# Four of sixteen window subtractions a step: from one GpSimd instruction to a negated copy and an accumulating DMA

## The reference

```python
disp = (x @ W_disp).reshape(B, T, nh, bd).transpose(0, 2, 1, 3)
disp_win = _windows(disp, delta)                        # delta = 64
strain = disp_win - disp[:, :, :, None, :]
bond_act = jax.nn.gelu(strain @ W_strain + rel_emb @ W_pos, approximate=False)
bond_logits = (bond_act @ W_bond)[..., 0]
damage_act = jax.nn.gelu(strain @ W_dmg + b_dmg, approximate=False)
damage = jax.nn.sigmoid((damage_act @ W_dmg_out)[..., 0] + b_dmg_out[0])
logits = bond_logits - 10.0 * damage
weights = jax.nn.softmax(logits, axis=-1)               # masked below the sequence's start
out = jnp.einsum('bntd,bntde->bnte', weights, val_win)
```

## Time and profile before

| | |
|---|---|
| median of three runs | 4021.71 us |
| the profiled execution | 4033.82 us, span 4032.3 us |
| VectorE busy | 3379.6 us, 84% of the span |
| ScalarE busy | 2576.9 us, 64% |
| TensorE busy | 2547.4 us, 63% |
| GpSimd busy | 2476.6 us, 61% |

### The profile page before, as it was taken

One profiled execution on the slowest core, in us unless ns is written; L12 is line 12 of the kernel. 1 busy time (PEld: TensorE's weight loads), 2 busy tenths in 40 slices (PEclk: granted clock), 3 DMA queues, 4 the chain that ended last, 5 costly groups with the idle time before them and its releaser, 6 DMA issues. The chain is left out here.

```text
span 4032.3 us, 64337 instructions
## 1 busy us (share of the span) xinstructions
PE 2547.4 (63%) x20970; PEld 1282.8 (32%) x20970; DVE 3379.6 (84%) x4350; ACT 2576.9 (64%) x1812; POOL 2476.6 (61%) x1748
## 2 busy tenths in 40 slices
PE   5661556766666666668888864565666656565556
PEld 3440112322222222246667631122222222222224
DVE  6886999999999999923433369999999999999993
ACT  1111878888788887833333356777777777777773
POOL 1222887668787787813333467677767767676762
PEclk9885878888888888879999987777878787878886
DMA  7883121322222222127887841222222222222222
GB/s 258 304 304 99 37 74 63 96 81 78 72 70 84 91 80 75 58 79 235 243 243 240 244 139 32 68 65 74 64 75 64 75 64 75 64 75 64 74 63 81
DMA packets 376227, 445.81 MB, mean 111 GB/s; under 512 B 49185, under 2 KB 291697, under 8 KB 376050
## 3 DMA queue, kind: packets, MB, share of 16 engines
q1 hardware_dynamic: 293106, 283.77, 22.4%
q0 software_dynamic: 58752, 148.46, 11.3%
q10 hardware_dynamic: 24192, 11.02, 1.0%
HBM read 239.08 MB, written 204.02 MB: 110 GB/s over the span
## 5 line engine op out<-in xcount | busy, mean ns | idle before, releaser
L1198 PE MATMUL ps_l<-u_dve,wsel 128*32 128x512 f32 x6144 | 1004.0, 780 | 1001.8 <-ACT u_dve L1003 640.7
L1102 DVE SCALAR_TENSOR_TENSOR u_dve<-s_win,rpos,ps_here 128x512 f32<-128x512 f32 x1792 | 1225.8, 737 | 74.3 <-PE ps_here L1181 51.4
L1003 ACT ACTIVATE u_dve<-u_dve 128x4096 f32<-128x4096 f32 x224 | 809.9, 3616 | 427.8 <-DVE u_dve L1102 427.0
L947 POOL TENSOR_TENSOR u_pool<-s_win 128x4096 f32<-128x4096 f32 x128 | 1021.9, 7983 | 9.7 <-PE ps_l L1198 6.9
L1097 DVE TENSOR_TENSOR u_dve<-s_win,ps_here 128x4096 f32<-128x4096 f32 x160 | 703.0, 4409 | 0.0
L1198 PEld LDWEIGHTS ps_l<-u_dve,wsel 128*32 128x32 f32 x6144 | 211.1, 128 | 1447.7 <-issue 647.1
L926 POOL DMA_INDIRECT xslot_dram<-xr,slot_now x512 | 520.0, 1016 | 154.1 <-issue 147.8
L935 POOL DMA_INDIRECT yg<-yslot_dram,slot_now x512 | 499.1, 975 | 164.6 <-issue 144.1
L1001 ACT ACTIVATE u_dve<-u_dve,bdmg_sb 128x4096 f32<-128x4096 f32 x128 | 474.6, 3708 | 91.5 <-DVE u_dve L1097 86.8
L1001 ACT ACTIVATE u_pool<-u_pool,bdmg_sb 128x4096 f32<-128x4096 f32 x128 | 473.7, 3701 | 27.7 <-POOL u_pool L947 27.5
L1391 DVE TENSOR_TENSOR hs<-sg,ps_e 128x512 f32<-128x512 f32 x168 | 115.4, 687 | 382.6 <-ACT sg L1376 382.6
(11 more groups left out here) (142 smaller groups left out, 3366.2 us busy)
## 6 DMA issues: line engine op xcount, KB each, us to landing
band<-band_dram SPq DMA_DIRECT2D x32, 2048.0 KB
xslot_dram<-zero SPq DMA_DIRECT2D x16, 2688.0 KB, 10.1
xs<-xslot_dram SPq DMA_DIRECT2D x168, 256.0 KB, 3.6
yslot_dram<-ys POOLq DMA_DIRECT2D x168, 256.0 KB, 3.2
band_dram<-ml SPq DMA_DIRECT2D x64, 512.0 KB
we<-in_w_expert SPq DMA_DIRECT2D x336, 64.0 KB, 2.8
s_win<-s_dram SPq DMA_DIRECT2D x64, 288.0 KB, 8.2
s_dram<-s_sb POOLq DMA_DIRECT2D x16, 1024.0 KB, 4.6
```

The source lines that it names most:

```text
L947: pool.tensor_tensor(item_buffer(n), windows(par, ty, d0, 8), s_win[:, par, ty, PAD:PAD + TC].unsqueeze(1).to_broadcast([P, 8, TC]), ALU.s ...
L1003: act.activation(u, u, ACT.Gelu).then_inc(gelu_done, 1)
L1102: last = dve.scalar_tensor_tensor(out=item_buffer(n)[:, d, :], in0=s_win[:, par, ty, d0 + d + 1:d0 + d + 1 + TC], scalar=rpos[:, d0 + d:d0 ...
L1198: last = pe.matmul(ps_l[32 * g:32 * g + 32, cgrp % 2, ty, :], wsel[:, ty, q, :], item_buffer(n)[:, d, :], start=(q == 0), stop=(q == 3))
```

## The change

GpSimd no longer subtracts. For items 3, 7, 11 and 15 it writes the negated own row 8 times into the item's buffer (a `tensor_scalar` with one SBUF input), waits for that write, and issues a DMA from SBUF to SBUF that adds the 8 shifted rows of `s_win` to what stands there. ScalarE waits for the DMA's semaphore instead of GpSimd's. The loads of the windows wait for `gelu_done` of the step before instead of the two subtraction counters. The rings keep their sizes (3 and 2).

```diff
-POOL_ITEMS = (3,)
+DMA_ITEMS = (3, 7, 11, 15)
+DVE_BUFS = 3
+DMA_BUFS = 2
...
-                            if some(ND * (2 * it + par - 1)):
-                                sp.wait_ge(sub_dve, ND * (2 * it + par - 1))
-                                sp.sem_inc(held, 1)
-                            if some(NPI * (2 * it + par - 1)):
-                                sp.wait_ge(sub_pool, NPI * (2 * it + par - 1))
+                            if some(NI * (2 * it + par - 1)):
+                                sp.wait_ge(gelu_done, NI * (2 * it + par - 1))
                                 sp.sem_inc(held, 1)
...
-                                pool.tensor_tensor(
-                                    item_buffer(n), windows(par, ty, d0, 8),
-                                    s_win[:, par, ty, PAD:PAD + TC].unsqueeze(1).to_broadcast([P, 8, TC]),
-                                    ALU.subtract).then_inc(sub_pool, 1)
+                                if some(NI * s + buffer_free(par, n)):
+                                    pool.wait_ge(item_done, NI * s + buffer_free(par, n))
+                                    pool.sem_inc(held, 1)
+                                u = item_buffer(par, n)
+                                pool.tensor_scalar(
+                                    u, s_win[:, par, ty, PAD:PAD + TC].unsqueeze(1).to_broadcast([P, 8, TC]),
+                                    -1.0, None, ALU.mult).then_inc(base_set, 1)
+                                pool.wait_ge(base_set, NM * s + k + 1)
+                                pool.sem_inc(held, 1)
+                                pool.dma_start(u, windows(par, ty, d0, 8), accum_op=ALU.add)\
+                                    .then_inc(sub_dma[landed(it, par, n)[0]], 16)
...
-                                if n % 4 in on_pool:
-                                    if some(NPI * s + pool_of[n]):
-                                        act.wait_ge(sub_pool, NPI * s + pool_of[n])
+                                if n in DMA_ITEMS:
+                                    i, count = landed(it, par, n)
+                                    act.wait_ge(sub_dma[i], count)
                                 else:
-                                    if some(ND * s + dve_of[n]):
-                                        act.wait_ge(sub_dve, ND * s + dve_of[n])
+                                    act.wait_ge(sub_dve, ND * s + dve_of[n])
```

More of the change, by code:

```diff
@@ L655, in moe_attention_layer @@
         win_loaded = [sem(f"win_loaded{g}") for g in range(HG)]
-        sub_dve, sub_pool, gelu_done, item_done = sem("sub_dve"), sem("sub_pool"), sem("gelu_done"), sem("item_done")
+        sub_dve, gelu_done, item_done = sem("sub_dve"), sem("gelu_done"), sem("item_done")
+        base_set, sub_dma = sem("base_set"), [sem(f"sub_dma{i}") for i in range(DMA_BUFS)]
         tanh_done, logits_in = sem("tanh_done"), sem("logits_in")
@@ L681, in attend @@
             chunk0 = (1 - half) * NCH // 2 - it0
-            u_dve = sb(f"u_dve_{half}", [P, 3, 8, TC], F32, c)
-            u_pool = sb(f"u_pool_{half}", [P, 2, 8, TC], F32, c)
+            u_dve = sb(f"u_dve_{half}", [P, DVE_BUFS, 8, TC], F32, c)
+            u_dma = sb(f"u_dma_{half}", [P, DMA_BUFS, 8, TC], F32, c)
             s_win = sb(f"s_win_{half}", [P, HG, 2, SW], F32, c)
@@ L709, in attend, with slot_of @@
             ps_u = c.enter_context(nc.psum_tensor(f"ps_u_{half}", [P, TC], F32))
[L710 to L714, removed]
+            on_dve = [n for n in range(NI) if n not in DMA_ITEMS]
+            dve_of = [sum(q in on_dve for q in range(n + 1)) for n in range(NI)]
+            ND, NM = len(on_dve), len(DMA_ITEMS)
+            def slot_of(m):
+                par, n = m // NI % 2, m % NI
+                if n in DMA_ITEMS:
+                    return "dma", (par * NM + DMA_ITEMS.index(n)) % DMA_BUFS
+                return "dve", (par * ND + on_dve.index(n)) % DVE_BUFS
             def steps(e, step):
@@ L738, in windows, with item_buffer, buffer_free, landed @@
                 return bass.AP(row.tensor, row.offset, [list(row.ap[0]), [1, nd], [1, TC]])
-            def item_buffer(n):
-                if n % 4 in on_pool:
[L743 to L750, removed]
+            def item_buffer(par, n):
+                which, i = slot_of(par * NI + n)
+                return (u_dma if which == "dma" else u_dve)[:, i]
+            def buffer_free(par, n):
+                m = par * NI + n
+                back = next(k for k in range(1, 2 * NI + 1) if slot_of(m - k) == slot_of(m))
+                return n - back + 1
+            def landed(it, par, n):
+                i = slot_of(par * NI + n)[1]
+                uses = [m for m in range(2 * NI) if slot_of(m) == ("dma", i)]
+                return i, 16 * (len(uses) * it + sum(m <= par * NI + n for m in uses))
             with nc.Block() as block:
@@ L1087, in step @@
                                     add_routed(s - first, 1 - par, 2 * n + d)
-                            if "i" in st and n % 4 not in on_pool:
+                            if "i" in st and n not in DMA_ITEMS:
                                 if dve_of[n] == 1:
@@ L1091, in step @@
                                     dve.wait_ge(here_done, s + 1)
-                                if some(NI * s + buffer_free(n)):
-                                    dve.wait_ge(item_done, NI * s + buffer_free(n))
+                                if some(NI * s + buffer_free(par, n)):
+                                    dve.wait_ge(item_done, NI * s + buffer_free(par, n))
                                 here = ps_here[:, ty, :]
                                 if ty or n in biased:
-                                    last = dve.tensor_tensor(item_buffer(n), windows(par, ty, d0, 8),
+                                    last = dve.tensor_tensor(item_buffer(par, n), windows(par, ty, d0, 8),
                                                              here.unsqueeze(1).to_broadcast([P, 8, TC]), ALU.subtract)
```

15 lines of the change are left out of this document (7 added, 8 removed).

## The result

The changed kernel takes 4600.19 us (median of 4 runs, 4591.94 to 4604.51), the kernel before takes 4021.43 us beside it: a ratio of 1.1442 [1.1426, 1.1458]. The forecast was 3883 us, its range 3777 to 4120; the kernel is slower by 14%, and slower than the range's end. Its profiled execution took 4604.27 us.

What follows compares the result with a forecast made beforehand. VectorE was taken to pace both halves. The profiled 4033.8 us - 245 (stalls) + 76 (half 1) + 29 (half 0) = 3894 us; the median runs 12 us lower, so 3883 was forecast, range 3777 to 4120.

Steps and rivals of the forecast that it cites:

- I take 3.6 us: the write has no second input to fetch, which puts it next to the memset: GpSimd's one-input write of 4096 elements, taken as 3.6 us, between a memset of 3.51 and the subtraction of 8.19.
- the 6 us that the prediction itself named as a sign of being wrong: A GpSimd write of over 6 us would show the forecast wrong.
- the write is no shorter: Rival, chance 0.06: GpSimd's write takes 7 to 8 us, stalls stay, landings come 4.4 us later; median 4197 us.
- The stalls: VectorE's two-input instructions wait 344 us for GpSimd's SBUF-reading instruction; the shorter write saves 71%, 245 us.
- The DMA: The accumulating DMA's time from issue to landing, L, taken as 16 us; upper bound near 23 us.
- lower bound: L if the second read is all that accumulation adds: 2.0 + 4 x 2.54 = 12.2 us.
- The estimate of 11.6 us: L from two skill pages, 2.0 + 9.6 us; with it the sum would be a gain of some 230 us.
- Right in mechanism in half 1: Late landing of item 3 delays VectorE's item 8 by 5.1 us in 15 steps of half 1: 76 us.
- the term "29 us": In even steps of half 0, item 7's late landing delays VectorE's item 12 by 4.1 us in 7 steps.
- GpSimd's DMA issues lie in the 4.6 us that its write gives back: Issuing the DMAs on GpSimd fits in the time its shorter write frees, so it costs nothing.
- VectorE's own stream was the same: VectorE's own instruction stream is unchanged by the edit, costed at nothing.
- late window: Window loads wait for Gelu, some 5 us later, costed at nothing; uncovered, VectorE's first item would start late by those 5 us.

Runs made afterwards that it cites:

- price list: Kernel before with single GpSimd operations on 128x4096 behind its end, each beside 8 VectorE additions: multiplication 11.0 us, copy 4.1, subtraction 7.5.
- no DMA: Changed kernel without the accumulating DMA, ScalarE waiting for GpSimd's write of the negated row: 4133.24 us, ratio 1.0279.
- late addition: Changed kernel with GpSimd's addition L978 at item 9 instead of item 5: 4518.68 us, ratio 1.1223.
- one item earlier: Each write and DMA issued one item earlier: changed kernel with its multiplication 4268.2 us; with the row negated once a step and copied 8 times 3736.85 us.
- the run in 4 pieces: Kernel before, no DMA, with GpSimd's subtraction cut into 4 instructions of 1024 elements: 4057.17 us, ratio 1.0116.
- the kernel with the copy: Changed kernel with a plain copy of the own row instead of the multiplication by -1: 3960.34 us, ratio 0.9849.

## Why the prediction was wrong

**The step that failed** is "I take 3.6 us: the write has no second input to fetch, which puts it next to the memset", with its bound above, "the two-input subtraction with 8.19 us". The write takes 10.6 us, outside both ends, and over the 6 us that the prediction itself named as a sign of being wrong. The bounds assumed that one input cannot cost more than two. The price list shows that it can: the kind of instruction decides (multiplication by a number 11.0 us, copy 4.1, two-input subtraction 7.5). The rival "the write is no shorter" had the direction, with a chance of 0.06 and a price of 4197; it priced later landings alone, with 8 us as the worst.

What the longer write does, as far as the runs show it, from the kernel before on:

- The write alone, 10.6 for 8.2 us: +114 us (no DMA), by way of stalls. The gates and the softmax line have 411.8 and 271.4 us there, 119 more than in the earlier trace rows; L1148 gives 42 back, and two lines that the prediction did not count, the mask's addition (L1131 before) and the copy of `slot_now`, add 45.
- The DMA behind it: 467 us more, by way of waits. In the changed kernel VectorE's idle time ahead of L1120 is 389.1 us, of which TensorE's late release is 288.7; the rest of its new idle time stands mostly ahead of the softmax (L1153 and L1160, 64 us each).
- Of this, the place of L978 is 82 us (late addition), and all that an earlier issue removes 332 us (4600 to 4268). What is left above the kernel before is 247 us: GpSimd's own program is longer than a step was, and the stalls don't shrink (in the profiled executions VectorE is busy 142 us longer than before and idle 93 us longer).

The multiplication in place of the copy makes 640 us in the old order (4600 to 3960) and some 530 one item earlier (4268 to 3737). These parts are differences between runs and overlap; they don't sum to a single account.

**The stalls.** Right: what holds VectorE is GpSimd's instruction that reads SBUF, and it is worth 328 us (344 worked out). That it holds for its whole length is right for the subtraction and the copy, and not for the new multiplication, which lets go 1.7 us before its end, after some 8.9 of 10.6 us. With a 3.6 us write 102 us stay (99 forecast). The "SBUF — State Buffer" page of the Trainium skill ("SBUF: two separate sides") has the lock held for a whole instruction and wanted only against a GpSimd instruction that reads SBUF. The second half agrees with the price list (4.90 us beside the memset, 8.30 beside the copy); of the first, the run in 4 pieces shows that the hold can outlast the instruction, when the next one follows at once, and the multiplication shows that it can be shorter.

**The DMA.** Right in size: 15.3 us from issue to landing, 16 taken, and 14.4 by itself. The working had a slip that changes little: the line through 4.6 us at 1 MB and 12.4 at 4 MB has a slope of 2.6 us a MB and not 2.54, so its lower bound is 12.4 and not 12.2 us. The estimate of 11.6 us from the Trainium skill ("Collectives: The Full Stack", section "The bandwidth ceiling: the fold count and why AG ≠ RS ≠ AR", with "DMA: Bandwidth & Descriptors", section "Anatomy of one DMA") was too low; the first of the pages states its halving for the reduce step of a ring of cores, which is near to this DMA and not the same. Right in mechanism in half 1: 79.2 us for 76, in the kernel with the copy. **In half 0 the term "29 us" was mis-sized**, and its path was wrong: it came to some 88 us. It followed one route (item 7, buffer of item 8, VectorE's item 12), and the late Gelu came out elsewhere, at the softmax steps that VectorE takes from ScalarE. With a write of the length forecast (the copy), the median was 3960 where the sum says 3883: right in sign and inside the range, with more than half of the gain gone (62 us for 139).

**Costed at nothing.** The DMA issues don't hold VectorE: right (4.90 us). "GpSimd's DMA issues lie in the 4.6 us that its write gives back": wrong, as the write gave nothing back; 128 issues of 1.7 us and the wait of 0.6 ahead of each are some 300 us more on GpSimd, on top of 334 us of longer writes. VectorE's own stream was the same: right. No wait of VectorE for a late window shows in the waits.

**What stays open.** Why the multiplication is slow: no run varied its type or its operation. Its cost goes with the number of elements: 512 take 1.5 us (the negated row, and the write of one row), 4096 take 10.6. Open too is which of the two, GpSimd's length or VectorE's stalls, sets the 247 us that stay with the earlier order, and what of the 82 us of the late addition is the circle.

## What to carry to other kernels

Price an instruction by its own kind before anything else: fewer inputs is no bound, and one run with a list of single operations on the shapes at hand settles it. When a step gets a longer latency, follow it to every engine that takes a result from the engine that waits, the writer itself included: one route to the pacing engine gives only a lower end. A latency that no buffer forbids to start earlier cost nothing here once its issue was moved one item ahead and the issuing engine had room (1.0 us of waits with the copy; with the multiplication 159.4 us stayed); and since moving work changes what stands beside what, the order alone should be run as a control.

## What the runs showed of the hardware

- GpSimd, 128x4096 float32: multiplication by a number 10.6 us in the kernel (11.0 beside VectorE in the list), two-input subtraction 7.3 to 8.2, copy 3.6 (4.1 in the list), memset 3.5.
- A VectorE instruction with two SBUF inputs stands to the end of GpSimd's subtraction (7.5 us) or copy (4.1 us), but only to 1.7 us before the end of its multiplication: 8 additions get longer by 6.8, 3.4 and 8.6 us, the last beside 11.0. A GpSimd instruction that follows at once keeps the hold: VectorE's L1140 stood 7.77 us through four subtractions of some 2.1 us. Beside a memset or a DMA issue the additions took 4.90 us, as undisturbed.
- A multiplication of 128x512 on GpSimd takes 1.5 us, one of 128x4096 10.6.
- A DMA that adds, 2 MB within SBUF in rows of 2 KB: 14.4 us from issue to landing and 1.71 us to issue; a plain one 9.2 and 0.93 us.
- DMA engines busy 0.87 of a stretch, and ScalarE waited 1.0 us in all for transfers that had been issued an item earlier.
